# Local attention's products with V as four 64x64 tiles of TensorE, and the copy of the turned weights on ScalarE in every slot

## What is computed

```python
def local_attention(q, k, v):            # w = 32, nw = 8 windows
    bk2, bv2 = look(bk), look(bv)        # the window before beside the own one: 64 keys
    sim = jnp.einsum('bhwie,bhwje->bhwij', bq, bk2) * QK_SCALE
    sim = jnp.where(mask, -jnp.finfo(sim.dtype).max, sim)
    attn = jax.nn.softmax(sim, -1)
    out = jnp.einsum('bhwij,bhwje->bhwie', attn, bv2)
    return out.reshape(b, h, n, d)
...
for i in range(DEPTH):                   # 6
    x = attn_layer(shift_tokens(x), ...) + x
    x = ffn_layer(shift_tokens(x), ...) + x
```

## Time and profile before

| | |
|---|---|
| median of 3 runs (1869.65 to 1872.12) | 1871.23 us |
| profiled execution, its own time | 1873.87 us |
| its span | 1872.1 us |
| PE busy | 1808.1 us, 97% |
| DVE busy | 1535.6 us, 82% |
| ACT busy | 1456.2 us, 78% |
| POOL busy | 1359.4 us, 73% |
| granted TensorE clock, mean | 0.998 |

### The profile page before, as it was taken

The page is one execution under the profiler, slowest core; times in us unless marked ns, Lnnn a source line. Parts: engine busy times, 40 slices in busy tenths (PEclk is TensorE's granted clock), DMA queues, the critical chain, the costliest instruction groups (busy, mean ns, idle before and its releaser), DMA issues.

```text
span 1872.1 us, 67927 instructions
## 1 busy us (share of the span) xinstructions
PE 1808.1 (97%) x26763; PEld 1370.4 (73%) x26763; DVE 1535.6 (82%) x3002; ACT 1456.2 (78%) x2976; POOL 1359.4 (73%) x1165
## 2 busy tenths in 40 slices
PE   6999998999999999999999999999999999999997
PEld 4777776777777777777777777777777777777774
DVE  5776777788889888888888888888888888888886
ACT  5766665678798888888887888778878878887884
POOL 3010023889889888888888898888888888888880
PEclk9999999999999999999999999999999999999999
DMA  3000001344343444334444434443344434444342
GB/s 111 1 1 0 0 25 28 91 114 116 104 110 100 112 113 111 97 103 110 114 112 104 105 102 115 113 107 101 103 106 122 112 98 103 111 104 103 98 103 69
DMA packets 200545, 171.01 MB, mean 91 GB/s; under 512 B 32400, under 2 KB 199480, under 8 KB 200248
## 3 DMA queue, kind: packets, MB, share of 16 engines
q1 hardware_dynamic: 200248, 166.89, 34.1%
HBM read 21.01 MB, written 1.05 MB: 12 GB/s over the span
## 4 chain that ended last, share of the span: by engine, by line
PE 61%; ACT 12%; DVE 11%; issue 7%; SPq 5%; POOL 4%; DMA 1%; ACTq 0%; DVEq 0%; POOLq 0%
PE bank L1011 6%; PE bank L1052 6%; PE bank L979 5%; PE pair_bank L1030 5%; PE bank L1062 4%; SPq L366 4%; PE bank L1114 3%; PE bank L1063 3%; PE bank L1064 3%; PE bank L1040 3%; PE bank L1136 3%; PE bank L897 2%; ACT sq L656 2%; DVE rot_v L1378 2%; PE bank L985 1%
## 5 line engine op out<-in xcount | busy, mean ns | idle before, releaser
L437 POOL TENSOR_TENSOR z_norm<-probs_t,z_raw 128x512 f32<-128x512 f32 x376 | 480.9, 1279 | 106.4 <-DVE probs_t L1459 104.2
L443 POOL TENSOR_TENSOR z_raw<-rot_u,rot_v 128x512 f32<-128x512 f32 x384 | 497.9, 1301 | 74.8 <-DVE rot_v L1378 72.0
L1377 DVE TENSOR_TENSOR rot_u<-bank,tabs 128x512 f32<-128x512 f32 x384 | 263.2, 685 | 175.8 <-ACT sq L656 174.6
L1062 PE MATMUL bank<-x_high,w_high 128*128 128x256 f32 x768 | 302.2, 394 | 0.0
L470 POOL TENSOR_TENSOR sqs<-sq 128x512 f32<-128x512 f32 x192 | 246.3, 1283 | 59.0 <-issue 57.9
L1378 DVE TENSOR_TENSOR rot_v<-bank,tabs 128x512 f32<-128x512 f32 x384 | 261.3, 681 | 0.0
L1052 PEld LDWEIGHTS bank<-probs_t,v_late 128*64 128x64 f32 x3072 | 155.0, 137 | 144.4 <-issue 144.4
L732 ACT ACTIVATE pair_bank<-pair_bank 128x512 f32<-128x512 f32 x192 | 111.7, 582 | 169.9 <-DVE pair_bank L1358 168.5
L656 ACT ACTIVATE sq<-bank 128x512 f32<-128x512 f32 x384 | 222.0, 593 | 24.2 <-PE bank L1064 17.7
L665 ACT ACTIVATE probs_t<-bank 64x512 f32<-64x512 f32 x340 | 200.9, 591 | 22.8 <-PE bank L1040 20.7
L1064 PE MATMUL bank<-x_low,w_high 128*128 128x256 f32 x768 | 216.4, 282 | 0.0
(11 more groups left out here) (190 smaller groups left out, 4538.6 us busy)
## 6 DMA issues: line engine op xcount, KB each, us to landing
zqk<-z_norm SPq DMA_DIRECT2D x1536, 64.0 KB, 2.1
v_late<-v_sb SPq DMA_DIRECT2D x192, 192.0 KB, 2.6
w_stage<-in_L_ffn_Wqkv SPq DMA_DIRECT2D x24, 384.0 KB, 3.6
v_late<-v_sb SPq DMA_DIRECT2D x192, 32.0 KB, 2.8
wo<-in_L_ffn_Wo SPq DMA_DIRECT2D x24, 128.0 KB, 2.4
w<-in_L_ffn_W SPq DMA_DIRECT2D x12, 170.5 KB, 3.1
z_norm<-in_L_attn_x SPq DMA_DIRECT2D x4, 256.0 KB, 5.3
out<-z_raw SPq DMA_DIRECT2D x4, 256.0 KB, 2.3
```

The source lines that it names most:

```text
L437: return pool.tensor_tensor(z_norm[:, parity, idx, :, :], rinv(m)[:, idx, :].unsqueeze(1).broadcast_to([P, 2, T]), z_raw[:, parity, idx, : ...
L443: pool.tensor_tensor(z_raw[:, parity, idx, :, :], rot_u[:, idx, :, :], rot_v[:, idx, ::-1, :], ALU.add).then_inc(S[mark], 1)
L1062: pe.matmul(dst, w_high[:, r, j, cols], x_high[:, odd, :], start=True, stop=False)
L1377: dve.tensor_tensor(rot_u[:, idx, :, :], src, tabs[:, 2 * idx, :, :], ALU.mult)
```

## The change

`spread` becomes one plain 128 x 512 copy without zeros, on ScalarE at every place (at place 1 it stands behind the gelus). `weigh_windows` splits each product by key half `x`: 32 products of 64 keys x 64 channels on 32 columns, at four tile positions (64x, 64a). The halves go to two banks, `B_PV = (bank 2, bank 4)`; bank 4 is also the queries' bank. So `weigh_windows` waits until the queries of the group before are taken (`q_prod`, `q_square`), `output_out` becomes two copies of 128 x 256 (`output_half`), and `queries` waits for the one that empties bank 4 (`lyt_half`). That copy stands between the Ln and the Exp of the norms. At place 0 `values` goes ahead of `queries`, and `values_out` ahead of the queries' squares.

```diff
-        spread = probs_t...[:, 0:HG * TILES * KEYS].rearrange("p (h s c) -> p h s c", h=HG, s=TILES)
+        spread = probs_t...[:, 0:HG * P]
+        B_PV = (bank[2], bank[4])
...
         # gpsimd slot
-                if s == 0:
-                    pool.wait_ge(S["pv_done"], STEPS)
-                    pool.memset(spread[:, :, :, :], 0.0).then_inc(S["spread_zero"], 1)
...
         # scalar
             def spread_out(n):
                 act.wait_ge(S["turned"], n + 1)
                 after(act, "lpv_done", n)
-                tiles = B_T.rearrange("p (h s c) -> p h s c", h=HG, s=TILES)
-                for x in range(2):
-                    rows = slice(KEYS * x, KEYS * x + KEYS)
-                    a = act.activation(spread[rows, :, :, WIN * x:WIN * x + WIN], tiles[rows, :, :, :], ACT.Copy)
-                a.then_inc(S["spread_ready"], 1)
+                act.activation(spread[:, :], B_T[:, :], ACT.Copy).then_inc(S["spread_ready"], 1)
...
-            def output_out(n):
+            def output_half(n, x, mark):
                 og = n % G
                 act.wait_ge(S["lpv_done"], n + 1)
                 after(act, "lwo_done", n + 1 - G)
-                act.activation(yt[:, 2 * og:2 * og + 2, :], B_T.rearrange("p (c t) -> p c t", c=2), ACT.Copy).then_inc(S["lyt_ready"], 1)
+                dst = yt[:, 2 * og:2 * og + 2, :].rearrange("p c (t x k) -> p c t x k", t=TT, x=2)[:, :, :, x, :]
+                act.activation(dst, B_PV[x][:, 0:T].rearrange("p (c t k) -> p c t k", c=2, t=TT), ACT.Copy).then_inc(S[mark], 1)
...
-                if four and not mlp_slot(s, 17):
+                if four:
                     spread_out(s - 1)
...
                     act.activation(ln_n(m), B_N..., ACT.Ln, ...).then_inc(S["ln_done"], 1)
+                if four:
+                    output_half(s - 1, 1, "lyt_half")
+                if two:
                     act.wait_ge(S["ln_done"], m + 1)
                     act.activation(rinv(m), ln_n(m), ACT.Exp, scale=-0.5).then_inc(S["rinv_ready"], 1)
                 if four:
-                    output_out(s - 1)
+                    output_half(s - 1, 0, "lyt_ready")
...
+                if mlp_slot(s, 16) and active(s + 1, -3, GROUPS - 3):
+                    values_out(s + 4)
                 if one:
                     squares(s + 4, "lq_done", B_Q, 0, "q_square")
...
                 if mlp_slot(s, 16):
-                    if active(s + 1, -3, GROUPS - 3):
-                        values_out(s + 4)
                     gelus((s - 16) // (2 * G))
...
         # tensor
             def queries(m):
+                after(pe, "lyt_half", m - 4)
                 project(m, 0, B_Q, m // G % 2, "lq_done", ("q_prod", "q_square"))
...
             def weigh_windows(n, unit, g, odd):
                 pe.wait_ge(S["spread_ready"], n + 1)
-                for pair, tile, a in itertools.product(range(2), range(TILES), range(2)):
+                after(pe, "q_prod", min(n + 5, GROUPS))
+                after(pe, "q_square", min(n + 5, GROUPS))
+                for pair, tile, x, a in itertools.product(range(2), range(TILES), range(2), range(2)):
                     h, t = 2 * pair + a, tile // 2
...
+                    at, of = P * pair + KEYS * t + WIN * (tile % 2), P * h + WIN * tile
+                    mm = pe.matmul(B_PV[x][D * a:D * a + D, at:at + WIN], (v_sb if tile % 2 else v_late)[rows, odd, t, f], spread[rows, of:of + WIN],
+                                   start=True, stop=True, tile_position=(KEYS * x, D * a), skip_group_check=True)
...
-                if one:
+                if one and mlp_slot(s, 16):
+                    values(s + 4, (s + 4) // G % 2)
+                    queries(s + 4)
+                elif one:
                     queries(s + 4)
-                if one:
                     values(s + 4, (s + 4) // G % 2)
...
         # vector
-            def spread_out(n):
...
-                if mlp_slot(s, 17) and active(s, 1, GROUPS + 1):
-                    spread_out(s - 1)
```

More of the change, by code:

```diff
@@ L160, in build @@
         scored = probs.rearrange("p h c -> p (h c)")[:, 0:HG * 2 * KEYS].rearrange("p (a k r) -> p a k r", a=2, r=KEYS)
-        spread = probs_t.rearrange("p h c -> p (h c)")[:, 0:HG * TILES * KEYS].rearrange("p (h s c) -> p h s c", h=HG, s=TILES)
+        spread = probs_t.rearrange("p h c -> p (h c)")[:, 0:HG * P]
         late_ln = probs.rearrange("p h c -> p (h c)")[:, 2 * GW * 2:].rearrange("p (a t) -> p a t", a=2)
@@ L201, in build @@
             n_done ln_done rinv_ready bound_ready zn_ready z_in0 z_in1 z_in2 z_in3 lv_ready v_late_in0 v_late_in1 v_late_in2 v_late_in3
-            scores_done mask_laid top_ready shifted raised sum_ready part_ready weights_ready turned spread_ready lpv_done lyt_ready
+            scores_done mask_laid top_ready shifted raised sum_ready part_ready weights_ready turned spread_ready lpv_done lyt_half lyt_ready
             wo_in0 wo_in1 wo_in2 wo_in3 lwo_done lres_done xc_done xc_ready xc_squared var_done ln_var rstd_ready xh_raw xh_ready
@@ L722, in slot @@
                 if s == 1:
-                    act.wait_ge(S["spread_zero"], 2)
-                if four and not mlp_slot(s, 17):
+                    act.wait_ge(S["pv_done"], STEPS)
+                if four:
                     spread_out(s - 1)
@@ L831, in _ @@
             deviations(W - 1, B_M)
-            output_out(N)
+            output_half(N, 1, "lyt_half")
+            output_half(N, 0, "lyt_ready")
             gained(W - 1)
@@ L1047, in weigh_windows @@
                 pe.wait_ge(S["spread_ready"], n + 1)
-                for pair, tile, a in itertools.product(range(2), range(TILES), range(2)):
+                after(pe, "q_prod", min(n + 5, GROUPS))
+                after(pe, "q_square", min(n + 5, GROUPS))
+                for pair, tile, x, a in itertools.product(range(2), range(TILES), range(2), range(2)):
                     h, t = 2 * pair + a, tile // 2
[L1050 to L1053, removed]
+                    f, rows = slice(g * GW + h * D, g * GW + (h + 1) * D), slice(KEYS * x, KEYS * x + KEYS)
+                    at, of = P * pair + KEYS * t + WIN * (tile % 2), P * h + WIN * tile
+                    mm = pe.matmul(B_PV[x][D * a:D * a + D, at:at + WIN], (v_sb if tile % 2 else v_late)[rows, odd, t, f], spread[rows, of:of + WIN],
+                                   start=True, stop=True, tile_position=(KEYS * x, D * a), skip_group_check=True)
                 mm.then_inc(S["lpv_done"], 1)
@@ L1083, in slot @@
                 if s == 1:
-                    pe.wait_ge(S["spread_zero"], 2)
+                    pe.wait_ge(S["spread_zero"], 1)
                 if four:
@@ L1218, in _ @@
             pe.wait_ge(S["q_square"], GROUPS)
+            pe.wait_ge(S["lyt_half"], GROUPS)
             for c in range(3):
@@ L1341, in by_block @@
                 return a[:, :, :].rearrange("p (a b) x -> p a (b x)", a=2)
-            def spread_out(n):
-                dve.wait_ge(S["turned"], n + 1)
-                after(dve, "lpv_done", n)
-                tiles = B_T.rearrange("p (h s c) -> p h s c", h=HG, s=TILES)
-                for x in range(2):
-                    rows = slice(KEYS * x, KEYS * x + KEYS)
-                    a = dve.tensor_copy(spread[rows, :, :, WIN * x:WIN * x + WIN], tiles[rows, :, :, :])
-                a.then_inc(S["spread_ready"], 1)
             def shift_windows(n):
```

## The result

The changed kernel takes **1907.91 us** (median of 4 runs, 1905.55 to 1909.3), the kernel before 1870.44 us on the same chip (1868.35 to 1872.12): 1.02 times as long, 95% interval 1.0182 to 1.0217. The forecast was 1891 us, with a range of 1858 to 1915. It is slower, as forecast, but by 37.5 us, not by 20. The profiled execution has a span of 1906.8 us, 34.7 more than the one before; that one lay 3.4 us above its kernel's median, this one 0.7, so the traces differ by less than the medians.

The account below looks back on a forecast made before the run. PE, busy 97%, was taken as the bound. Waits of 5.0 + 5.9 + 16.4 = 27.3 us less 7.1 of block gain gave +20.2, so profiled 1873.87 became 1894, forecast as a 1891 us median; range 1858 to 1915.

Parts of the forecast that it names:

- loads that hinder each other: Rival on the weighing block: four positions loading 64 channels slow each other, block 1.30 us, total 1924 us; chance 0.09.
- the forecast's own range: Main case for the whole kernel: 1880 to 1903 us, with block gain 0 to 0.12 us; chance 0.55.
- The block's gain, 7.1 us: Weighing block on PE: 1.08 us falls to 1.02, 0.06 us gained in each of 118 blocks that count.
- The first four loads of the block, two on each position, take 0.11 us to the next four: Weighing block of the kernel before: reading that gave 55 ns for a load of 64 channels.
- Place 0 to place 1, 16.4 us: ScalarE's chain between these slots of a full eight-slot round: Ln 0.95 us later, mean loss 0.75 us over 22 rounds.
- ends over a microsecond ahead of the weighing: Spread copy on ScalarE: said to finish early enough that PE's weighing never waits, priced at nothing.
- the queries' wait, forecast at about 1 us: Place 1: PE's queries were to wait about 1 us for ScalarE's half copy, standing behind a later Ln.
- Places 6 and 7: Slots where an MLP product between weighing and queries was to cover the half copy's wait; no loss priced.
- VectorE's bound: VectorE's wait for the norms' Exp, up to 0.4 us later: said to stand behind VectorE's own work, priced at nothing.
- Covered where the Ln is early: Places 1 to 4, 6, 7: the half copy needs 0.67 us after the weighing, hidden behind an MLP product of 0.95 us.
- Place 5, 5.9 us: Queries wait for the half copy behind a late Ln: 0.16 us lost, 0.6 with rotary tables, mean 0.27 over 22 rounds.
- The early slots, 5.0 us: Twelve slots without MLP product: queries right behind the weighing wait 0.62 us for the half copy, counted in eight.

Follow-up runs that it names:

- experiment 3: Changed kernel with the spread copy of place 1 back on VectorE as one 128 x 512 copy: 1897.82 us, 1.0143 times the kernel before.
- experiment 4: Changed kernel with the norms' Exp ahead of the first half copy again at place 0 of the full rounds: 1898.26 us, 1.0148 times the kernel before.
- experiments 1 and 2: Changed kernel at places 6 and 7: first, gate copies ahead of the keys' squares, 1895.42 us; second, norms' Exp ahead of the first half copy, 1895.91 us.
- the kernel with eight positions: Changed kernel with each product with V split again into two of 32 channels, 64 products on eight array positions: 2024.7 us, run once.

## Why the prediction was right, and where it was off

- **The direction and its reason: right.** Loads set the block's pace, the change gives PE new waits for ScalarE, and nothing pays for them. That 1907.91 lies within the range is in part luck: the range's upper end, 1915, was drawn for loads that hinder each other, and the forecast's own range ended at 1903; a late gate copy was in neither.
- **The block's gain, 7.1 us: mis-sized.** The step was "The first four loads of the block, two on each position, take 0.11 us to the next four", from which it took 55 ns for a load. In the steady part a load takes 58 ns; the old step was 58.5 already, so it stood on the loads before too. The gain is 0.01 us (1.08 to 1.07), not 0.06. The rule of the Trainium skill that the prediction weighed ("TensorEngine Tiling (Array Packing)", section "Instruction Overhead": a matmul of 1 column lasts as long as one of 60) foretold the unchanged block, and streams of 64 columns do cost what 32 do (1.08 and 1.07); but with 32 channels the same streams of 32 columns pass in 0.69 us, so it is not the columns' floor that holds the block. What does agree is the Trainium skill's "TensorE: Matmul & The Clock Gate", section "LDWEIGHTS (loading the stationary operand)": a load takes the time of its columns at 1.2 per ns, whatever its rows. By that section of the Trainium skill 64 columns make an estimated 53 ns, near the 58 here, and 64 rows in place of 128 changed nothing.
- **Place 0 to place 1, 16.4 us: right.** 0.48 for the spread copy was 0.49 (experiment 3), 0.47 for the Exp 0.38 (experiment 4), and PE's old wait of 0.42 at place 2 swallowed 0.43: 15.7 us over the rounds. Places 1 and 2 together lost 0.90 to 0.94 us in 15 of the 22 rounds, where 0.95 was forecast, and nothing in four of the five in which PE waited for POOL at place 2, where 0.25 was forecast. That the spread copy "ends over a microsecond ahead of the weighing" was wrong at place 1: behind the gelus it made PE wait 0.62 us there, and the queries' wait, forecast at about 1 us, is 0.42. The 0.62 lies beside the queries' wait and costs nothing of its own.
- **Places 6 and 7: the failed step.** "an MLP product lies between weighing and queries" and "Covered where the Ln is early" hold for the queries. But the list of those who wait for ScalarE behind its new wait ended with the queries and VectorE's bound. The gate copy stands in the same queue, five places behind, and bank 3 is needed again at the end of the slot; at place 7 its reader had nothing to spare. These two places cost 12.3 us, a third of the loss, and experiments 1 and 2 each gave 12 us back.
- **Place 5, 5.9 us: too high, 2.0.** In the five rounds with rotary tables it lost 0.61 to 0.63, as worked out (0.6); in the others nothing in place of 0.16 (the first round gained 0.91). The half copy ended at 1413.81 and the queries began at 1413.86, so a ScalarE end costs PE 0.05 us there, not the 0.15 taken.
- **The early slots, 5.0 us: right in sum**, 4.1 net, and partly by luck. The wait was to be 0.62 us in eight of the twelve; it stands in all twelve, at 0.50 to 0.53, since here too the queries start 0.05 us behind the copy, and nine of the slots lost 0.24 to 0.57 us. **The tail**: slots 190 and 191 lost 1.1 and 1.0, which the prediction did not price.

## What to carry to other kernels

Splitting the products into more tiles shortened nothing here, since a position kept the number of its loads and their channels: count those first. Where an engine gets a new wait, go through every instruction queued behind it up to the end of the slot and ask for each how much time its reader had to spare; the costly one here was five instructions further on, in another bank. Work that is ready belongs ahead of a wait: the Exp ahead of the half copy alone gave back 12 us at two places and 10 at a third.

## What the runs showed of the hardware

With 128 records a block, PE stopped within the weighing 42 times, 44.7 us together, with no wait that the profile names; the changed kernel has two such gaps (1.7 us), the kernel before none. One of them, on PE's timeline of the kernel with eight positions:

```profile
1177.81 0.23 PE L1055 MATMUL bank<-probs_t,v_late 64*32 64x32 f32 x3 [2.36 <-issue]
...
1178.12 2.07 PE L1131 MATMUL bank<-xh,w 128*128 128x512 f32 x2
```

The windows around it (us, busy us of PE, PEld, DVE, ACT, POOL, granted clock, DMA share, GB/s):

```profile
1174.20:1178.10 3.90, 1.54 (x128) 1.38 (x128) 1.83 (x4) 2.25 (x3) 2.49 (x4) 0.98 0.38 104
1178.10:1181.20 3.10, 3.10 (x17) 2.04 (x9) 1.93 (x4) 2.18 (x5) 1.27 (x1) 0.50 0.34 81
```

PE stood for 2.36 us within a block of small records, and for the next 3.1 us the granted clock was 0.50, the level of 1.2 GHz: a product of 1.13 us took 2.07. The page's queue of instructions (packets, MB, share) stands at

```profile
q8 instruction: 351, 5.75, 1.3%
```

where it moved 4.18 MB in the changed kernel and 3.38 before. The trace's DMA records go further: in all 42 stops, and in the two of the changed kernel, PE went on 1.2 to 1.7 us after a packet of this queue (16 KB each) had ended; for the stop shown the packet ran from 1175.36 to 1176.25 us. A moment picked at random stands so in about one case in ten. So PE very likely waited for its program, though no run tests it. The stops (43 us more than in the changed kernel) and 0.37 us more a block in 192 slots (71 us, if each counts in full) make 114 of the 117 us that this kernel takes more than the changed one.
